# Turning adj in blocks of 128 by 1024 in two places instead of 128 by 512 in four, beside an attention layer bound by TensorE

## The reference, cut to what matters

```python
scores = einsum('hnd,hmd->hnm', qh, kh) * SCALE + graph_bias * adj   # 4 heads
scores = where(adj == 0, -1e9, scores)
x = layernorm(x + softmax(scores) @ v @ Wout + bout)                 # layer 0
x = layernorm(x + softmax(where(adj > 0 | eye, leaky_relu(...), NEG)) @ Wh)   # layer 1
x = layernorm(x + adj_norm @ x @ W.T + b)                            # layer 2
x = layernorm(x + relu(adj_norm @ x @ W))                            # layer 3
```

## Time and profile before

| what | value |
|---|---|
| median of 3 runs | 3140.5 us (3138.62 to 3140.7) |
| the profiled execution | 3139.6 us, its span 3137.9 us |
| busy share of the span | PE 96%, PEld 69%, DVE 67%, ACT 60%, POOL 27% |
| mean granted TensorE clock | 0.989 |
| DMA | 530.50 MB, 722,509 packets, 566,640 of them under 512 B |

### The profile page before, as it was taken

The page is one execution under the profiler, slowest core; times in us unless marked ns, Lnnn a source line. Parts: engine busy times, 40 slices in busy tenths (PEclk is TensorE's granted clock), DMA queues, the critical chain, the costliest instruction groups (busy, mean ns, idle before and its releaser), DMA issues.

```text
span 3137.9 us, 45405 instructions
## 1 busy us (share of the span) xinstructions
PE 3011.7 (96%) x16612; PEld 2177.2 (69%) x16612; DVE 2101.2 (67%) x3604; ACT 1896.6 (60%) x2705; POOL 850.2 (27%) x467
## 2 busy tenths in 40 slices
PE   8999999999999999999998999999989999699998
PEld 6677777777777777777775555555558888578886
DVE  6777777777777777777756977777435554465564
ACT  3677777777777777777774677777543333343332
POOL 2124431344223442234401455544400000000000
PEclk9999999999999999999999999999999999899999
DMA  6689999998999989898946333332279998689982
GB/s 185 142 172 184 185 197 170 173 185 182 194 166 176 185 188 185 167 178 187 193 86 258 119 128 141 121 140 102 55 169 213 215 203 197 151 192 217 209 197 55
DMA packets 722509, 530.50 MB, mean 169 GB/s; under 512 B 566640, under 2 KB 602480, under 8 KB 705904
## 3 DMA queue, kind: packets, MB, share of 16 engines
q1 hardware_dynamic: 679728, 440.55, 60.9%
q10 hardware_dynamic: 36288, 66.08, 11.6%
q0 software_dynamic: 6272, 20.98, 2.1%
HBM read 439.36 MB, written 88.08 MB: 168 GB/s over the span
## 4 chain that ended last, share of the span: by engine, by line
PE 80%; DVE 10%; DMA 3%; issue 3%; ACT 2%; SPq 2%; POOL 1%; DVEq 0%; POOLq 0%; ACTq 0%
PE at_score L529 15%; PE at_o L554 12%; PE gl_four L1356 11%; PE at_turn L541 11%; PE gl_quad L1406 7%; PE gl_quad L1407 7%; PE gl_quad L1408 7%; DVE at_probs L781 4%; PE gl_quad L1339 3%; PE at_mixed L563 2%; DMA gl_early<-x 2%; PE gl_four L1381 2%; DVE at_bias L747 2%; SPq L1166 1%; PE at_mixed L512 1%
## 5 line engine op out<-in xcount | busy, mean ns | idle before, releaser
L781 DVE CUSTOM_DVE_ANT_0 at_probs<-at_score,at_bias 128x1024 f32<-128x1024 f32 x509 | 621.2, 1220 | 387.0 <-PE at_score L529 383.9
L668 ACT ACTIVATE at_pT<-at_turn 128x1024 f32<-128x1024 f32 x512 | 521.2, 1019 | 276.4 <-PE at_turn L541 274.7
L529 PE MATMUL at_score<-at_kT,at_q 128*128 128x512 f32 x2036 | 610.9, 422 | 34.3 <-DVE at_maxima L781 34.3
L659 ACT ACTIVATE at_probs<-at_probs,at_minus_max 128x1024 f32<-128x1024 f32 x512 | 586.0, 1144 | 64.3 <-DVE at_minus_max L786 63.4
L455 POOL TENSOR_SCALAR at_masked<-at_bias 128x512 bf16<-128x512 f32 x240 | 482.6, 2032 | 444.0 <-DMA at_bias<-in_adj 344.7
L554 PE MATMUL at_o<-at_pT,at_values 128*64 128x256 f32 x4096 | 498.4, 386 | 0.0
L541 PE MATMUL at_turn<-all_ident,at_probs 128*128 128x128 f32 x4096 | 489.0, 273 | 0.0
L541 PEld LDWEIGHTS at_turn<-all_ident,at_probs 128*128 128x128 f32 x4096 | 462.4, 140 | 35.4 <-issue 1.5
L1356 PE MATMUL gl_four<-gl_early,gl_first_wh 128*128 128x512 f32 x1024 | 464.0, 596 | 12.1 <-ACT gl_early L1474 12.1
L529 PEld LDWEIGHTS at_score<-at_kT,at_q 128*128 128x128 f32 x2036 | 351.8, 189 | 152.5 <-DVE at_maxima L781 82.9
L1406 PE MATMUL gl_quad<-gl_split,gl_rows_hi 128*128 128x512 f32 x1024 | 407.1, 398 | 27.6 <-DVE gl_split L1687 27.6
(11 more groups left out here) (122 smaller groups left out, 2951.8 us busy)
## 6 DMA issues: line engine op xcount, KB each, us to landing
gl_units<-adjT SPq DMA_DIRECT2D x512, 256.0 KB, 8.4
at_bias<-in_adj SPq DMA_DIRECT2D x128, 512.0 KB, 6.5
at_probs<-in_adj SPq DMA_DIRECT2D x256, 256.0 KB, 5.1
adjT<-at_probs SPq DMA_DIRECT2D x1024, 64.0 KB, 4.5
gl_first_weights<-in_adj SPq DMA_DIRECT2D x32, 2048.0 KB, 8.2
at_values<-v_heads ACTq DMA_DIRECT2D x252, 256.0 KB, 4.8
gl_early<-x SPq DMA_DIRECT2D x24, 512.0 KB, 4.6
x<-gl_early POOLq DMA_DIRECT2D x16, 512.0 KB, 4.4
```

The lines of the kernel that those rows point to most:

```text
L529: last = pe.matmul(place[:, at], q[:, q_place(h), part, t * P:(t + 1) * P], kT[:, h, col:col + BANK], start=part == 0, stop=part == 1)
L659: act.activation(part, part, ACT.Exp, bias=minus_max[:, k, t:t + 1], scale=1.0, accum_out=sums[:, k, t, pp:pp + 1]).then_inc(prob_ready, 1)
L668: act.activation(pT[:, j % PT_SLOTS, :], turn_bank[j % 2][:], ACT.Copy).then_inc(pT_ready, 1)
L781: dve.tensor_tensor_reduce(out=ring[:, place_in_ring(u, pp), t, :], in0=place[:], in1=bias[:, t, at], scale=SCALE, scalar=LOWEST, op0=ALU. ...
```

## The change

Blocks are 128 by 1024, in two places. There are 128 blocks, nine in a chunk, in beats 0, 4, 7, 11, 14, 18, 21, 25 and 28; the last one is turned in beat 4 of the last chunk but one. A load is 512 KB in rows of 4 KB, a store 128 KB, still in runs of 128 bytes. One block is loaded ahead of the first beat, and after the stores of block b, SP issues the load of block b+1. The layout of `adjT` and the space in SBUF stay the same.

```diff
-        self.block_stored = [space.sem(f"block_stored{k}") for k in range(4)]
+        self.block_stored = [space.sem(f"block_stored{k}") for k in range(2)]
...
-    BLOCK = 4 * P
+    BLOCK = 8 * P
     BLOCK_TILES = 4
...
-    BLOCK_PLACES = 4
+    BLOCK_PLACES = 2
...
-    BLOCK_BEATS = (0, 2, 4, 6, 8, 10, 12, 14, 15, 17, 19, 22, 24, 27, 28, 30, 31)
+    BLOCK_BEATS = (0, 4, 7, 11, 14, 18, 21, 25, 28)
...
-                to = adjT.rearrange("j (s k r) -> j s k r", k=BLOCK_TILES * SQUARES, r=BLOCK)
+                to = adjT.rearrange("j (s k r) -> j s k r", k=BLOCK // SQUARE, r=BLOCK_TILES * P)
...
-            for b in range(3):
-                load_block(b)
+            load_block(0)
...
-                        if b + 3 < BLOCKS:
-                            wait(sync, block_stored[(b + 3) % BLOCK_PLACES], 16 * SQUARES * ((b + 3) // BLOCK_PLACES))
-                            load_block(b + 3)
+                        if b + 1 < BLOCKS:
+                            wait(sync, block_stored[(b + 1) % BLOCK_PLACES], 16 * SQUARES * ((b + 1) // BLOCK_PLACES))
+                            load_block(b + 1)
```

## The result

The changed kernel takes 3609.4 us, median of 4 runs (3590.7 to 3617.9), beside 3140.6 for the kernel before: a ratio of 1.1485, 95% interval 1.1438 to 1.1531. It is slower, as forecast, but by 469 us where 137 were forecast, and above the range that ended at 3390. The profiled execution took 3590.65 us, its span is 3588.9.

The account below looks back on a forecast made before the run. TensorE was taken to set the pace, its scores waiting for VectorE. 14 chunks x (1.6 us for VectorE's beats + 8.3 for late loads) = 138.6; 3139.6 + 138.6 - 1 = 3277 us, range 3172 to 3390.

Parts of the forecast that it names:

- TensorE sets the pace of layer 0: One chunk of layer 0: TensorE busy 97.2 of 99.1 us; its scores wait for VectorE, which works in order.
- The price of a transpose: On VectorE, a transpose of 1024 columns was taken as 1.23 us, against 0.703 for 512 columns.
- VectorE's beats: Longer transposes in other beats of VectorE make TensorE's scores wait: 1.6 us more a chunk.
- The load is issued only behind the stores: Load of block b+1 follows block b's stores and must land before VectorE's next transpose; called the large term.
- the cycle: Time from the end of a transpose to the landing of the next block's load; 6.9 us taken for half-size blocks.
- The cycle becomes 10.2 us: Per block: 6.9 + 2.7 for stores + 0.7 for the load = 10.3 us, used as 10.2; 11.6 in beats 12 to 20.
- More: 2.7 us: Stores of a block: 4096 packets at 21 ns take 5.4 us of all 16 engines, before 2048 and 2.7.
- all doubles: Upper bound of the cycle, 13.8 us, if everything in it doubles with the block; the lower bound was 6.9.
- rival 1: DMA engines bind the cycle: stores queue, 12 us in every interval, chunk 119 us, time 3420 us; chance 14%.
- Four of nine intervals wait: VectorE stands still before transposes in beats 7, 14, 21 and 28 for the load; the chunk grows by 8.3 us.
- rival 2: Only the volume counts: stores and load at 43.5 engine-us per MB, a cycle of 8.3 us, time 3183 us; chance 14%.
- The fit that the forecast names: The skill's DMA time, 2 us plus bytes at 436 GB/s: the doubled block would add 1.2 us to the cycle.

Follow-up runs that it names:

- long_runs: The changed kernel with each partition's 1024 numbers stored as one run of 4 KB, 128 packets a block instead of 4096: 3179.3 us in one run.
- wide_all_four: The changed kernel with the load ahead of the stores, eight 64 KB stores split by columns, and rows padded by 4 KB: 3178.4 us, ratio 1.0113.
- small_ahead_one: The kernel before, blocks of 512 in four places, but each load issued one block ahead, behind the stores of the block before: 3665.2 us in one run.

## Why the prediction was right in its direction and wrong in its size

- *TensorE sets the pace of layer 0, and VectorE's in-order queue is the way by which a late load reaches it.* Right, by the chain and by 413.8 us of TensorE's waits.
- *The price of a transpose.* Right: 1.242 us for 1.23.
- *VectorE's beats, 1.6 us a chunk, 22 in all.* (The waits of the bias beats add up to 3.7 there, not 3.8, so 1.5 a chunk.) Right in size as far as the runs show. In long_runs and wide_all_four TensorE stands still 25.6 and 30.5 us longer in layer 0, up to 13 and 4 of it for loads, so some 12 to 27 are left for VectorE's order. What the forecast lacked is that TensorE also took 12.8 and 12.0 us longer for the same work; the last part of this section says where that lies.
- *The load is issued only behind the stores, and the cycle sets the chunk.* Right; this is the mechanism, and small_ahead_one shows it without wide blocks.
- *The cycle becomes 10.2 us.* This is the step that failed: the term "More: 2.7 us" for the stores. It was priced at 21 ns a packet, from a stretch in which DMAs of 512 runs went out, and took the price as one of the packet. It depends on what is written together. A DMA of twice the columns writes over twice the stretch of every row, and 4096 packets took about 12 us and not 5.4. The bound above, 13.8 us ("all doubles"), was close: 13.9 in the turn of the chain shown. That it was close is luck; it doubled the issues and the load as well, and the issues stayed at 2.3 us. That bound makes a chunk of 9 x (13.8 + 1.23) = 135 us and a time of 3139.6 + 14 x 36 = 3644 us, but the range ended at 3390, short even of rival 1. It named the bound and then did not carry it into the range.
- *Four of nine intervals wait.* Wrong, following from this: 86 of 128 transposes waited, and in the chunk shown eight of nine did. That is rival 1's picture (chance 14%), with a cycle of 13.2 us on average (130.0 / 9 - 1.24) where it had 12. Its reason was that the DMA engines bind the cycle. They are full indeed (a share of 1.12 in the chunk, below), but wide_all_four moves the same nine blocks a chunk with a median landing of 4.7 us for the load: what fills the engines is how the stores are cut and where they write, not how much there is to move.
- *Going by the row, and not by rival 2.* Right: rival 2's 3183 is 426 us short. The rule of the Trainium skill that larger transfers are better ("DMA: Bandwidth & Descriptors", section Bandwidth) spoke for rival 2. For the long runs it fits: 128 KB stores landed in 2.3 us. For these stores the larger DMA was the slower one, 7.7 us, and two of half the size were faster, 3.5 each. The fit that the forecast names stands in that page's section "Anatomy of one DMA — SWDGE (gpsimd) path" and is for DMAs that GpSimd issues; SP issues these.
- *The pitch of 2 MB.* The forecast did not weigh it. The Trainium skill, "DMA: Bandwidth & Descriptors", section "Latency and other measured facts", reports that rows a large power of two apart slow DMA copies and that 4 KB more restore them; its figures are for copies of 16 KiB rows between tensors in memory. The traces agree in direction (7.7 to 5.8 us and 4.5 to 3.6 us), but here the padding restored only a part.

**TensorE's clock** is a second, smaller part that the forecast left out. The chunk's row of the changed kernel, against the earlier trace rows:

```profile
1018.82:1155.00 136.18, 111.77 (x714) 81.06 (x710) 77.60 (x139) 77.27 (x114) 33.57 (x18) 0.92 1.12 139
```

(The DMA share of 1.12 is over one because packets of a queue overlap in time.) The mean granted clock is 0.92, not 1.00, so part of the time lies at the lower of its two levels, 1.2 GHz. TensorE's timeline shows where: behind its longer waits.

```profile
1050.25 2.08 PE L528 MATMUL at_score<-at_kT,at_q 128*128 128x512 f32 x4 [6.37 <-DVE at_maxima L780]
1052.26 3.06 PE L553 MATMUL at_o<-at_pT,at_values 128*64 128x256 f32 x16
```

The same scores take 1.20 us and the same products 1.95 elsewhere in the chunk, so this one wait of 6.4 us costs 2.0 us more behind it. Over the span TensorE is busy 3135.7 us for the work of 3011.7. How much of these 124 us lies on the path I didn't isolate. In wide_all_four, where few loads are waited for, the same is seen on a smaller scale: behind a wait of 2.8 us that ends at 1086.95 us, the products take 3.22 us for 1.95, and layer 0 has 12.0 us more of busy time.

What stays open is what makes those addresses dear. Not tried were stores from another engine's queue, and wide blocks in three places. The runs show that the spacing within a row, the pitch of the rows and the way a block is cut into DMAs all count, and that at the same count of packets the landing of a store goes from 3.4 to 7.7 us.

## What to carry to other kernels

A buffer ring with fewer places is a change of order first: ask for each load what must be finished before it is issued, and add up that loop from the chain's rows; if it is longer than the interval between uses, it is the new period. Price a DMA with short runs by its addresses and not by its bytes or packets; a row of 16 busy engines at 40 GB/s is the sign, and padding a power-of-two pitch or cutting the DMA along its long stretch is cheap to try. Where the bounds of an unknown cost lie far apart and the time is steep in it, the range must reach to the dear end.

## What the runs showed of the hardware that I had not expected

- One 128 KB store of 1024 runs of 128 bytes landed in 7.7 us with the runs 2 KB apart, in 5.8 with the rows' pitch padded by 4 KB, and in 3.4 with the runs 512 bytes apart; as runs of 4 KB in 2.3.
- Cutting it in two by columns (3.5 us each, the kernel at 3437 us) is much better than by partitions (5.0 us, 3564), beside 3609 uncut.
- The collapse sets in within a burst: 190 GB/s in its first microsecond, then a mean of 43 over 7.5 us.
- Behind a wait of 6.4 us, TensorE took 2.08 us for what else takes 1.20, and then 3.06 for 1.95, before it was back at 1.20.
